# Wide products with unread columns and two 256-column products a step, with the attention done inside the recurrence by ten steps

## The reference

```python
x_proj = einsum('btd,gd->btg', x, W_ih) + b_ih + b_hh
def step(carry, xp):                       # 6250 times, one after the other
    gates = xp + h @ W_hh.T                # 1024 gates
    i, f, g, o = split(gates, 4)
    c = sigmoid(f) * c + sigmoid(i) * tanh(g)
    h = sigmoid(o) * tanh(c)
logits = einsum('bth,lh->btl', lstm_out, W_lin) + b_lin      # 2 classes
g = argmax(logits)                         # 0 or 1 for each row
w = g * lstm_out
inc = cumsum(w, axis=1)                    # a running sum over the 6250 rows
prefix = inc - w
suffix = inc[:, -1:, :] - inc
return 2.0 * lstm_out + prefix * fw_att + suffix * bw_att    # added to x
```

## Time and profile before

| | before |
|---|---|
| median of the timed runs | 13971.03 us |
| profiled execution: time, span | 13987.69 us, 13985.9 us |
| mean granted TensorE clock | 0.549 of 2.4 GHz |
| busy: PE, PEld, DVE, ACT, POOL | 72%, 65%, 62%, 37%, 15% |
| stages before the recurrence | 0 to 2998 us |
| recurrence | 2998 to 13826 us |
| attention and output | 13826 to 13986 us |

### The profile page before, as it was taken

One profiled execution on the slowest core, in us unless ns is written; L12 is line 12 of the kernel. 1 busy time (PEld: TensorE's weight loads), 2 busy tenths in 40 slices (PEclk: granted clock), 3 DMA queues, 4 the chain that ended last, 5 costly groups with the idle time before them and its releaser, 6 DMA issues. The chain is left out here.

```text
span 13985.9 us, 721250 instructions
## 1 busy us (share of the span) xinstructions
PE 10063.6 (72%) x285273; PEld 9131.5 (65%) x285273; DVE 8604.1 (62%) x65379; ACT 5184.4 (37%) x32393; POOL 2070.5 (15%) x1598
## 2 busy tenths in 40 slices
PE   3444444687777777777777777777777777777776
PEld 2333333567777777777777777777777777777775
DVE  4444222256666666666666666666666666666667
ACT  1111111144444444444444444444444444444443
POOL 5888788400000000000000000000000000000000
PEclk8666777865555555555555555555555555555556
DMA  6555455410000000000000000000000000000001
GB/s 164 91 90 90 80 83 83 92 34 1 1 1 1 1 1 1 1 1 1 1 1 1 1 1 1 1 1 1 1 1 1 1 1 1 1 1 1 1 1 19
DMA packets 2057504, 301.47 MB, mean 22 GB/s; under 512 B 1894943, under 2 KB 2013747, under 8 KB 2056843
## 3 DMA queue, kind: packets, MB, share of 16 engines
q0 software_dynamic: 150048, 204.90, 9.0%
q1 hardware_dynamic: 1896678, 91.09, 8.1%
q10 hardware_dynamic: 10742, 5.06, 0.1%
HBM read 153.07 MB, written 141.27 MB: 21 GB/s over the span
## 5 line engine op out<-in xcount | busy, mean ns | idle before, releaser
L1422 PE MATMUL bank<-hp,whh 128*128 128x1 f16 (+1 forms) x225000 | 7000.0, 166 | 2320.7 <-DVE hp L1553 2320.7
L1422 PEld LDWEIGHTS bank<-hp,whh 128*128 128x128 f16 x225000 | 6488.6, 104 | 2864.1 <-DVE hp L1553 2863.6
L1500 ACT ACTIVATE gates<-last_banks 128x3 f32<-128x3 f32 x12500 | 2085.4, 174 | 6161.2 <-DVE last_banks L1538 6161.2
L1538 DVE TENSOR_REDUCE last_banks<-bank 128x3 f32<-128x6 f32 x12500 | 2076.6, 172 | 2393.9 <-PE bank L1422 2393.9
L1422 PE MATMUL bank<-xsteps,wih 128*128 128x10 f16 (+1 forms) x45036 | 2331.0, 170 | 0.0
L1542 DVE CUSTOM_DVE_ANT_1 uv<-gates 128x4 f32<-128x4 f32 x12500 | 2019.4, 164 | 506.3 <-ACT gates L1500 0.2
L1553 DVE TENSOR_TENSOR_SCAN hp<-last_banks,opening 128x2 f16<-128x2 f32 x12500 | 1968.9, 161 | 569.1 <-ACT last_banks L1509 108.7
L1509 ACT ACTIVATE last_banks<-gates 128x1 f32<-128x1 f32 x12500 | 2085.2, 174 | 0.1
L1422 PEld LDWEIGHTS bank<-xsteps,wih 128*128 128x128 f16 x45036 | 1917.6, 104 | 0.0
L1558 DVE TENSOR_TENSOR_SCAN hp<-last_banks,hp 128x2 f16<-128x2 f32 x12500 | 1759.2, 159 | 0.0
L1629 POOL TENSOR_TENSOR U<-U (+1 forms) x25 | 27.5, 1139 | 11171.2 <-POOLq L1572 11171.2
(11 more groups left out here) (184 smaller groups left out, 3199.8 us busy)
## 6 DMA issues: line engine op xcount, KB each, us to landing
xsteps<-x_d SPq DMA_DIRECT2D x1252, 5.0 KB, 1.8
U<-hp SPq DMA_DIRECT2D x1250, 5.0 KB, 2.5
acc_d<-zero SPq DMA_DIRECT2D x30, 640.0 KB, 12.9
ht<-acc_d SPq DMA_DIRECT2D x75, 224.0 KB
rows<-xn_d,staged_i POOLq DMA_INDIRECT x782
acc_d<-sums,target POOLq DMA_INDIRECT x782, 3.8
xi<-xn_d SPq DMA_DIRECT2D x50, 125.0 KB
xi<-in_x SPq DMA_DIRECT2D x50, 125.0 KB
```

The source lines that it names most:

```text
L1422: return nc.tensor.matmul(to, w, v, start=start, stop=True, skip_group_check=True)
L1500: nc.scalar.activation(gates[:, k, 0:6:2], zi[k], ACT.Tanh, scale=down)\
L1538: nc.vector.tensor_reduce(zi[k], gi[k][b][:, s], axis=AX.X, op=ALU.add).then_inc(ifg_summed[k], 1)
```

## The change

- **Wide products.** The moving operand of a product is read again and again (a stride of zero), so that the product has more columns; the added columns land in parts of the PSUM bank that nobody reads. `rest_of_weights`: 16 columns in place of 1. `weights(m, 0)`: 32 in place of 2; `weights(m, 1)` stays at 2. `output_gates`: 48 in place of 1. Every product of `projection`: 30 in place of 5 or 10. The number of products stays: 36 a step and 44 in five steps.
- **Spare products.** `spare_columns` multiplies a block of weights with 256 columns of whh into a part of a bank that nobody reads: two of them at the end of each step (one in the two steps that hold the class logits), and 48 ahead of the first step. They are written behind the products of the projection, and TensorE takes them in order.
- **The projection's 44 products** are shared out as 12, 3, 3, 12, 14 over the five steps instead of 9, 9, 9, 9, 8.
- **The attention goes into the recurrence.** For each ten steps, while the next ten run, VectorE does 11 short instructions behind `state2` (`join` and `follow`): it joins the states (10 columns for each half k), adds twice the state to XT, chooses the class, weighs, runs the sum, and adds the two products to XT. TensorE makes the class logits with 32-bit products in the steps b = 0, s = 1 and 2; ScalarE adds the bias at the end of step s = 2. The store of the states to U (L1398) and the wait for it go.
- **The last stage** has one pass: ScalarE adds one vector to XT (the last sum times bw), TensorE transposes, VectorE copies, SyncE stores.
- The small vectors are loaded at the start of the second normalisation and prepared at its end.

```diff
+            GATE_COLS, OUT_COLS = B * 3 * PARTS, B * KD
+            gi_wide = [[bank[2 * k + b][:, 0:GATE_COLS * 16].rearrange("p (j n) -> p j n", n=GATE_COLS) for b in range(2)]
+                       for k in range(KD)]
+            go_wide = [bank[4 + b][:, 0:OUT_COLS * 48].rearrange("p (j n) -> p j n", n=OUT_COLS) for b in range(2)]
+            NX = 6
+            def again(v, times):
+                return v.rearrange("p (o t) -> p o t", o=1).broadcast_to([128, times, v.shape[-1]])
...
-                        for k in range(KD):
-                            sp.wait_ge(h2_ready[k], (2 * i + b + 1) * B)
-                            sp.sem_inc(sp_turn)
-                        sp.dma_start(Hs[:, bass.ds((2 * i + b) * B, B), :], h_pairs[:, b * B:(b + 1) * B, :, 1]).then_inc(h_out[b], 16)
...
+                share = (12, 3, 3, 12, 14)
+                def spare_columns(b, start=False):
+                    return matmul(bank[2 + b][:, 256:512], wih[:, 0, 0, 0:128], whh[:, 0, 0, 0:256], start)
+                for n in range(48):
+                    spare_columns(1, start=n == 0)
+                def class_logits(i, l):
+                    if l == 0:
+                        pe.wait_ge(after, AFTER * i - AFTER + 2)
+                    for k in range(KD):
+                        last = nc.tensor.matmul(logits[l], wlb[:, k, l, :], hj[:, k, :], start=k == 0, stop=k == KD - 1,
+                                                skip_group_check=True)
+                    if l:
+                        last.then_inc(l_made, 1)
...
                     def rest_of_weights(m, k):
                         for g in range(3):
-                            product(gi[m][b][:, s, g, 0:1], 1, k, g, m, FIRST)
+                            product(gi_wide[m][b][:, :, col(s, g):col(s, g) + 1], 1, k, g, m, FIRST)
                     def weights(m, k):
                         for g in range(3):
-                            last = product(gi[m][b][:, s, g, :], 0, k, g, m, BOTH)
+                            to = gi[m][b][:, s, g, :] if k else gi_wide[m][b][:, :, col(s, g):col(s, g) + PARTS]
+                            last = product(to, 0, k, g, m, BOTH)
...
+                    if b == 0 and due(i):
+                        if s == 0:
+                            pass
+                        elif s <= 2:
+                            class_logits(i, s - 1)
+                        elif s == 4:
+                            pe.wait_ge(after, AFTER * i - AFTER + 4)
+                    n = share[s]
                     for m in state["ahead"][:n]:
                         last = matmul(*m)
+                    for _ in range(1 if b == 0 and s in (1, 2) else 2):
+                        last = spare_columns(1 - b)
...
                     def state1(k):
                         dve.wait_ge(tc_ready[k], t + 1)
-                        if s == 0 and due(16 * i):
-                            dve.wait_ge(h_out[b], 16 * i)
...
                     state2(1)
+                    if b == 1 and s == 0:
+                        join(i, 0, t)
+                    elif due(i):
+                        follow(i, b * B + s, t)
+                def follow(i, at, t, last=False):
+                    first = AFTER * i - AFTER
+                    cols = bass.ds(i * (2 * B) - 2 * B, 2 * B)
+                    if at == 0:
+                        join(i, 1, t)
+                    elif at == 1:
+                        dve.wait_ge(after, first + 2)
+                        stt(out=XT[:, :, cols], in0=hj[:], scalar=2.0 / (1 << H_EXP), in1=XT[:, :, cols], op0=ALU.mult,
+                            op1=ALU.add).then_inc(after, 1)
+                    elif at == 3:
+                        dve.wait_ge(l0_ready, i)
+                        stt(out=gate[:], in0=logits[1], scalar=bl[:, 1:2], in1=l0[:], op0=ALU.add, op1=ALU.is_gt)\
+                          .then_inc(after, 1)
+                    elif at == 4:
+                        dve.wait_ge(after, first + 4)
+                        nc.vector.tensor_tensor(wgt[:], hj[:], gate[:].rearrange("p (o n) -> p o n", o=1)
+                                                .broadcast_to([128, KD, 2 * B]), ALU.mult).then_inc(after, 1)
+                    elif at in (6, 7):
+                        dve.wait_ge(after, first + 5)
+                        k = at - 6
+                        nc.vector.tensor_tensor_scan(inc[:, k, :], one[:], wgt[:, k, :], inc[:, k, 2 * B - 1:2 * B],
+                                                     ALU.mult, ALU.add).then_inc(after, 1)
+                    elif at in (8, 9):
+                        k = at - 8
+                        stt(out=XT[:, k, cols], in0=wgt[:, k, :], scalar=minus_fw[:, k:k + 1], in1=XT[:, k, cols],
+                            op0=ALU.mult, op1=ALU.add).then_inc(after, 1)
+                        dve.wait_ge(after, first + (8 if last else 9) + 2 * k)
+                        stt(out=XT[:, k, cols], in0=inc[:, k, :], scalar=diff[:, k:k + 1], in1=XT[:, k, cols],
+                            op0=ALU.mult, op1=ALU.add).then_inc(after, 1)
...
                 def body(c, n, b):
+                    at = bass.ds(c * C, C)
                     if due(c - 1):
-                        act.wait_ge(fin_ready, c - 1)
+                        act.wait_ge(fin_turned, c - 1)
                     for k in range(KD):
-                        nc.scalar.activation(suf[:, b, k, :], inc[:, k, bass.ds(c * C, C)], ACT.Identity,
-                                             scale=diff[:, k:k + 1], bias=lastw[:, k:k + 1]).then_inc(suf_ready, 1)
+                        last = nc.scalar.activation(fin[:, b, k, :], XT[:, k, at], ACT.Identity, bias=lastw[:, k:k + 1])
+                    last.then_inc(fin_ready, 1)
```

More of the change, by code:

```diff
@@ L139, in gps_layer_kernel @@
         unscale = sb("unscale", [128, 1], I32)
+        wl = sb("wl", [128, KD, 2])
+        wlb = sb("wlb", [128, KD, 2, 128])
+        bl = sb("bl", [128, 2])
+        fw, bw, diff, minus_fw = (sb(n, [128, KD]) for n in ("fw", "bw", "diff", "minus_fw"))
+        one = sb("one", [128, 2 * B])
+        inc = sb("inc", [128, KD, 2 * B])
+        lastw = sb("lastw", [128, KD])
+        att_in, lastw_ready = sem("att_in"), sem("lastw_ready")
         ZW = (N + SPARE) * D // 128 // ZS
@@ L1348, in gps_layer_kernel @@
             hp = sb("hp", [128, 2 * B, KD, 4], F16, st)
-            h_pairs = hp[:].rearrange("p t k c -> p (t k c)").bitcast(F32).rearrange("p (t k c) -> p t k c", k=KD, c=2)
+            hj = sb("hj", [128, KD, 2 * B], F32, st)
+            l0 = sb("l0", [128, 2 * B], F32, st)
+            gate = sb("gate", [128, 2 * B], F32, st)
+            wgt = sb("wgt", [128, KD, 2 * B], F32, st)
+            logits = [bank[5][:, 484 + 14 * l:484 + 14 * l + 2 * B] for l in range(2)]
+            AFTER = 11
             opening = sb("opening", [128, 2], F16, st)
@@ L1369, in gps_layer_kernel @@
             ifg_act, o_act, c_ready, tc_ready = pair("ifg_act"), sem("ogate_act"), pair("c_ready"), pair("tc_ready")
-            h_out = [sem(f"h_out{b}") for b in range(2)]
+            after, l_made, l0_ready = sem("after"), sem("l_made"), sem("l0_ready")
             XW = KD * B * PARTS
@@ L1489, in _ @@
                 steps(pe, body)
+                for l in range(2):
+                    class_logits(NI, l)
             @block.scalar
@@ L1515, in body, with first_logit @@
                     tanh_cell(1)
+                    if b == 0 and s == 2 and due(i):
+                        first_logit(i)
+                def first_logit(i):
+                    act.wait_ge(l_made, i)
+                    nc.scalar.activation(l0[:], logits[0], ACT.Identity, bias=bl[:, 0:1]).then_inc(l0_ready, 1)
                 act.wait_ge(tanh0, 1)
@@ L1519, in _ @@
                 steps(act, body)
+                first_logit(NI)
             @block.vector
@@ L1568, in body, with join @@
                     state2(1)
+                    if b == 1 and s == 0:
+                        join(i, 0, t)
+                    elif due(i):
+                        follow(i, b * B + s, t)
+                def join(i, half, t):
+                    for k in range(KD):
+                        dve.wait_ge(h2_ready[k], t)
+                    at = slice(half * B, half * B + B)
+                    nc.vector.tensor_tensor(hj[:, :, at], hp[:, at, :, 2].rearrange("p t k -> p k t"),
+                                            hp[:, at, :, 3].rearrange("p t k -> p k t"), ALU.add).then_inc(after, 1)
@@ L1570, in _ @@
                 steps(dve, body)
+                for at in (0, 1, 3, 4, 6, 7, 8, 9):
+                    follow(NI, at, N, last=True)
+                dve.wait_ge(after, AFTER * NI)
+                nc.vector.tensor_tensor(lastw[:], bw[:], inc[:, :, 2 * B - 1], ALU.mult).then_inc(lastw_ready, 1)
         stage.close()
         with ExitStack() as st:
-            wl = sb("wl", [128, KD, 2], F32, st)
-            wlb = sb("wlb", [128, KD, 2, 128], F32, st)
```

(1 more changed line is left out.)

184 lines of the change are left out of this document (46 added, 138 removed).

## The result

The changed kernel takes 14696.49 us (median of 4 runs, 14695.61 to 14698.32), against 13969.15 us of the kernel before: ratio 1.052, 95% interval 1.0502 to 1.0538. It is 5.2% slower; I had forecast 3.5% faster. (Both medians are of four runs; the 13971.03 us ahead of the prediction is that of the first three.) The profiled execution has a span of 14,694.0 us.

A forecast was written before the change was run, and what follows sets the result against it. Bound: the recurrence's circle of products and VectorE at 1.2 GHz, no engine full. Terms -625 - 56 + 281 - 120 + 7 + 30 = -483 gave span 13,503, forecast 13,488 us, 3.5% faster; range 13,190 to 13,880.

The forecast's parts named there:

- (a): TensorE's products in the recurrence: wide products bring 2.4 GHz, pace and latency save 0.10 us a step, 625 us.
- Cover: Part of the clock term: output gates end later by nothing; projection, spare products and logits are hidden at 2.4 GHz.
- the third rival: Clock stays low, wide products paid in full at output gates and step end: about 15,490 us; 12%.
- the first rival: Only the latency gets shorter; 26.7 ns between weight loads is TensorE's instruction rate: 13,863 us; 22%.
- (b): Wait for the store, once in ten steps at `state1`: register instruction and second wait go, 0.09 us each time, 56 us saved.
- (c): VectorE's 11 new instructions between `state2` and next sum: late only at at = 8 and 9, 0.45 us together, 281 us lost.
- (d): From the last state to the end: 163 us becomes 43, 120 us saved.
- (e): The beginning: 48 spare products ahead of step 0 cost 7 us; small loads and VectorE's preparation cost nothing.
- (f): Short dips to 1.2 GHz, above all around the two steps with logits: 30 us lost.
- The clock stays low: Rival at output gates and step end: 1.2 GHz stays, wide products paid in full, about 15,490 us; 12%.

The follow-up runs named there:

- out16_spare3: Changed kernel with output gates at 16 columns instead of 48 and one more spare 256-column product in each step: 13,953.38 us, 0.9974 of the kernel before.
- out16_spare2: out16_spare3 with two spare products a step (one in the steps with logits) as in the change: 14,044.26 us, one run.
- the probe's rows: Changed kernel plus rows of 12 or 16 products of one form ahead of the first step, to time columns; no total time given.
- out_narrow: Changed kernel with the 12 output-gate products of a step back at 1 column, all else as changed: 14,787.72 us, 1.0574 of the kernel before.
- attention_only: Changed kernel with all products as narrow as before and no spare products: 14,233.80 us, 1.0185 of the kernel before.

## Why the prediction was wrong

**The step that failed** is in (a), under *Cover*: "The output gates end later by nothing: 12 x 20 ns is less than 12 x 26.7." They take 12 x 44 ns. I had read the price of a column from products of 10 and of one (172 against 166 ns; that is 0.67 ns, and the 0.9 of my range stands on no row), about one array cycle, and carried it to columns of another kind: read again and again and written apart. The two-cycle price stands in none of the earlier trace rows, and I gave it no bound at all; the part ought to have carried at least twice the cycle. I did have the mechanism, an output gate's tanh that pushes the cell's back by about 0.13 us, in the third rival, but tied to 1.2 GHz. It came at 2.4 GHz, at 0.15 us. It moved 0.15 x 6250 = 940 us, of a miss of 1208 (14,696 - 13,488); most of the rest is (a), next.

**(a) pace and latency**, forecast -0.10 us a step. The pace went from 26.7 to 25 ns, not to 13.3: the first rival, with the Trainium skill's 25 ns. The latency gain of 0.03, taken from 250-column products, is not there for narrow ones (165 to 163 ns). Together 0.02 in the change; with 48 columns out of the way the step is 1.70, and 1.685 with narrow first products: 0.04 at most. In the change that is 0.08 x 6250 = 500 us short of the forecast; the turn, below, gave 190 of it back. The clock itself was right: 1.00 in the loop. (The 1.84 and 1.09 us that I called weight loads are in the earlier trace rows the products behind them; the loads took 1.76 and 1.06, nearly the same ratio. That ratio did not carry over to the 16-bit loads.)

**(b) and (c), VectorE's work.** Place and mechanism were right: nothing at the steps with one instruction, nothing at the first chained pair, the price at the turn. The size was 0.355 us in out16_spare3 against 0.40, in the change about 0.145, since the output gate's wait hid a part; together with the wait for the store (0.09, gone as forecast) it is +32 us, not +225.

**(d) the end**: 49 us against 43 forecast, 114 saved and not 120. A size within 6 us.

**(e), (f)**: the 7 us at the beginning do not show (0.15 us; among the kernels of this study the first sum starts anywhere from 2997 to 3019 us); the dips forecast at 30 us are not in the change, but in out16_spare3 and out16_spare2 they are.

**The rivals.** "The clock stays low" had 12%, and its state did not come. Its 15,490 us rest on the same column price: with 80 ns for 48 columns and about 50 ns for the projection's 30 at 1.2 GHz, its ten steps would come to some 26 us and not 19.6 (an estimate from the probe's rows). out_narrow shows a low clock at 14,788 us, but with output gates of one column and at 0.59, between the two levels on average. My chance of 0.17 for slower rested on the clock, and the slower outcome came without it.

## What to carry to other kernels

A product that is widened to keep the clock up has a price by the form of its columns, and where it stands on the path a probe of a dozen such products is worth more than a column price from another form. Before paying for a higher clock ask which of the waits it shortens: here the pace of weight load and product, at 25 ns, hardly moved, and the clock was worth 0.02 to 0.04 us of 1.72 in a step, and 0.17 more in the steps with 32-bit products. Work that is put into an engine's idle time must stay clear of the step ahead of a loop's turn, where the turn already uses the idle time. One thing was not tried: ScalarE's tanh of the cell written ahead of that of the output gate, so that late output gates would not hold it.

## What the runs showed of the hardware

- Columns that are one column read again and again, or that are written 10 numbers apart, take about two array cycles each (48 of them: 41 to 45 ns at 2.4 GHz; one read again and written apart, 80 at 1.2); 48 different columns written densely take one or less (25 ns at 2.4 GHz, 40 at 1.2). Two neighbouring columns read again and again and written as pairs, 32 in all, still follow each other at 25 to 26 ns at 2.4 GHz (`weights(m, 0)` in the change).
- A 16-bit weight load with its narrow product takes 26.7 ns at 1.2 GHz and 25 at 2.4. Dense products of 256 columns follow each other at 108 to 109 ns at 2.4.
- From the start of VectorE's last instruction ahead of the loop's turn to the start of the first behind it are 0.50 us, with 0.27 idle, in out16_spare3 (8012.23 to 8012.73), in attention_only and in the change (8013.99 to 8014.49). In the first two the idle time is put down to "issue", so no wait shows it.
